# An attention kernel stores 1/std in rows turned by DVE, and each transfer of a step waits for a mark of its own

## The chip, the cores and the metric

The kernel runs on one core of a Trainium2 chip. The metric is the device time of one execution, in microseconds (us). TensorE is called PE here, VectorE DVE, ScalarE ACT, GpSimd POOL, and SyncE SP; SP only issues transfers.

## What is computed

`x` has 16 sequences of 1024 tokens with 512 features. It is layer-normed, and the result goes into two branches that are added to `x`: a state-space block in chunks of 64 tokens ("attention"), and a mixture of experts in which, for each group of 32 tokens, each expert and set takes the token with the largest logit.

```python
xn = _layernorm(x)                       # (x - mean) / sqrt(var + 1e-5)
# attention branch
proj = xn @ W_in.T                       # xp, z (512 each), B, C (256 each), dt_low (16)
dt = softplus(dt_low @ dt_W.T + dt_b)
dAcs = cumsum(dt * -exp(A_log))          # within a chunk of 64
scores = einsum(C, B) * exp(dAcs_i - dAcs_j) * causal * dt_j
y = scores @ xp + C @ state * exp(dAcs) + xp * D_param   # state carried over chunks
y = y / rms(y) * norm_w * silu(z)
attn = y @ W_out.T
# expert branch, in groups of 32 tokens
logits = xn @ Wc + bc + tie
perm = logits == max over the group      # one token for each of 32 x 4 experts and sets
inner = relu(picked @ W1 + b1)
ffn = spread(inner @ W2 + b2, perm)
out = x + attn + ffn
```

## The kernel before

Three phases run one after the other, joined at their edges: attention (to about 2300 us of the span), gather (picked tokens and W1, to about 2740 us), and scatter (W2, spreading, sum). The change touches the attention phase alone.

**Steps.** The 16384 tokens are 128 tiles of 128 tokens (index n), taken two at a time in 64 steps (s, `NST`) of 256 tokens. A loop over s from 0 to 65 is written out by hand once for each engine. It works on three steps at once: step s is projected, step s - 1 scanned, and step s - 2 gated and projected out (n0 = 2s, n1 = 2(s - 1), n2 = 2(s - 2)); the first half of an iteration treats the first tile of each, the second half the second.

**1/std.** Layer norm is folded in: the projections run on the raw `x`, turned on the host (`xT`, loaded to `xr` and split into a high and a low float32r part, `xT`, by ACT `hi_x` and DVE `lo_x`), against weights whose column means were taken away at the start (`column_means`, `centre`), and their results are multiplied by 1/std on the way out of PSUM. DVE takes the statistics of a tile (`stats`, `finish_stats`), POOL makes 1/std of them (`inv_std`, four small operations, into a column of `rs`), and ACT `normalize` writes the normed tile `xn`, which SP stores for the gather phase. The logits come out with tokens along the free axis, so they need 1/std as a row on every partition: SP stores the two columns of a step to DRAM (`store_rs`, L326, token by token), waits for that to land, and loads it back to all partitions (`load_rsb`, L331). DVE `picks` (L791) uses it at the end of the step.

**PE's order in an iteration** (`tensor_program`, L1034 on): two `project_bdt` (24 matmuls together), transposes of B, `project_x(n0)`, transposes of yz, chunk states and scores of n1 (128 and short), `project_z(n0)`, `project_out(n2)`, `sums`, `scan(n1)` (L989, recorded as 128 matmuls of 32 columns, with as many weight loads); then the same for the second tiles, with `project_c` and `project_logits`, up to `scan(n1 + 1)`. The first scan waits for DVE `mask_scores(n1)` (L736) and for ACT and POOL `spread_c`.

**The rest of the iteration.** DVE: `scale_y`, `expand_c`, `gate`, `lo_x`, statistics, `lo_yz`, `states`, `mask_scores`, `residual`, `states`, and again for the second tile, then `picks(s)`. ACT: copies of the projections, `hi_x(s + 1)`, softplus, `copy_x`, `spread_c`, `normalize`, `silu_z`, `square`. POOL: `add_skip`, `inv_std`, `spread_c`, `skip_x`, `inv_rms`, `scale_b`.

**SP's order.** SP issues every transfer of the loop, in program order, and stops at each wait. The lines (L366 to L382) give: xr(s + 2), when `lo_x(s)` is done; the store of rs(s + 1); the store of xn; the store of part 0 of step s - 2, after its residual; the load of an x tile; then the load of rsb(s + 1); the store of the other xn; the store of perm, which waits for `picks(s)`; the store of part 1; and the load of the other x tile.

Of the kernel before, what the change touches and what calls it, by code (L numbers as in the profile page):

```python
# [24 lines left out]
ALU = mybir.AluOpType  # L25
# [66 lines left out]
def attention_phase(nc, io, keep, sems):  # L92
# [49 lines left out]
    rs = sb("rs", [P, NT])  # L142
# [63 lines left out]
    rs_out = sem("rs_out")  # L206
# [48 lines left out]
    rs_cols = keep["rs"].rearrange("s i p -> s p i")  # L255
# [60 lines left out]
    def sync_program(sync, gather):  # L316
# [4 lines left out]
        def load_xr(s):  # L321
            sync.dma_start(xr_place(s), io["xT"][s]).then_inc(xr_in[s % 2], 16)

        def store_rs(s):
            sync.wait_ge(ln_pool, 4 * (2 * s + 1) + 2)
            sync.dma_start(rs_cols[s], rs[:, 2 * s:2 * s + 2], allow_slow_non_contiguous=True).then_inc(rs_out, 16)  # L326

        def load_rsb(s):
            sync.wait_ge(rs_out, 16 * (s + 1))
            wait(sync, pm, 4 * (s - 2) + 1)  # L330
            sync.dma_start(rsb[:, s % 2, :], rs_rows[s].partition_broadcast(P)).then_inc(rsb_in[s % 2], 16)  # L331

        for t in range(2):
            sync.dma_start(x[:, t, :], x_dram[t]).then_inc(x_in[t], 16)
        for n, (src, _) in enumerate(stages):
            if n == 2:
                for dst, name in consts[4:]:
                    sync.dma_start(dst[:], io[name]).then_inc(const_in, 16)
# [3 lines left out]
            if n == 2:  # L342
                load_xr(0)
                sync.dma_start(x[:, 2, :], x_dram[2]).then_inc(x_in[2], 16)
                for t in range(2):
                    store_xn(t, t)
                store_rs(0)
            if n >= 2:
                sync.wait_ge(w_lo, n - 1)
            sync.dma_start(stage_view(n), src).then_inc(w_in[n % 2], 16)  # L350
        for t in range(3, 4):
            sync.dma_start(x[:, t, :], x_dram[t]).then_inc(x_in[t], 16)

        store_xn(2, 0)
        load_rsb(0)
        sync.wait_ge(w_lo, LAST_STAGE)
        load_xr(1)

        for s in range(NST + 2):
            if s == NST:  # L360
                sync.wait_ge(lg_ps, NST)
                gather["load_w1"](sync, 0)
# [3 lines left out]
            for i in range(2):  # L366
                if i == 0 and valid(s + 2):
                    sync.wait_ge(xT_lo, s + 1)
                    load_xr(s + 2)
                if valid(s + 1):  # L370
                    (store_rs, load_rsb)[i](s + 1)
                if valid(s + 1 + i):
                    store_xn(2 * (s + 1 + i) + 1 - i, 1 - i)
                if i == 1 and valid(s):
                    sync.wait_ge(pm, 4 * s + 4)
                    sync.dma_start(perm_dram[s], permT[:, s % 2, :]).then_inc(pm_out[s % 2], 16)
                if valid(s - 2):
                    sync.wait_ge(res_cp, 2 * (s - 2) + i + 1)
                    sync.dma_start(part_dram[2 * (s - 2) + i], res[:, i, :].rearrange("p (k c) -> p k c", k=KD)).then_inc(res_out[i], 16)
                if valid(s + 2):  # L380
                    n = 2 * (s + 2) + i
                    sync.dma_start(x[:, n % (2 * STB), :], x_dram[n]).then_inc(x_in[n % (2 * STB)], 16)  # L382

    def gpsimd_program(pool, gather):
        for col, value in ((ones, 1.0), (mhalf, -0.5), (ln_eps, LN_EPS), (mean, 1.0 / D)):
            nc.gpsimd.memset(col[:], value).then_inc(zeroed, 1)
        pool.wait_ge(zeroed, 4)

        def inv_std(n, j):
# [5 lines left out]
            nc.gpsimd.tensor_tensor(rs[:, n:n + 1], ve[:, j:j + 1], mhalf[:], ALU.pow).then_inc(ln_pool, 1)  # L395
            nc.gpsimd.tensor_scalar(nm[:, j:j + 1], mv[:, j, 0:1], -1.0, 1.0, ALU.mult, ALU.mult).then_inc(ln_pool, 1)
            pool.wait_ge(ln_pool, 4 * n + 3)
            nc.gpsimd.tensor_tensor(nb[:, j:j + 1], nm[:, j:j + 1], rs[:, n:n + 1], ALU.mult).then_inc(ln_pool, 1)
# [82 lines left out]
        pool.wait_ge(zeroed, 7)  # L481
        pool.wait_ge(a_ready, 2)
        inv_std(2, 0)
        gather["negate_b1"](pool)
        for s in range(NST + 2):
# [6 lines left out]
            if valid(s + 1):  # L492
                inv_std(2 * (s + 1) + 1, 1)
# [14 lines left out]
            if valid(s + 2):  # L508
                inv_std(2 * (s + 2), 0)
# [5 lines left out]
    def scalar_program(act, gather):  # L515
        def hi_x(s):
            act.wait_ge(xr_in[s % 2], 16 * (s // 2 + 1))
# [3 lines left out]
        def normalize(n):  # L521
# [3 lines left out]
                                 scale=rs[:, n:n + 1]).then_inc(xn_ready, 1)  # L525
# [28 lines left out]
        normalize(2)  # L554

        gather["cast_ident"](act)

        def copy_bdt(n):
# [3 lines left out]
            nc.scalar.activation(raw[:, n % 4, :], proj[n % 2][:, 0:C_C], ACT.Copy, scale=rs[:, n:n + 1]).then_inc(bdt_cp, 1)  # L562
# [5 lines left out]
        def copy_x(n):  # L568
# [3 lines left out]
            for c in range(2):  # L572
                rows_ = token_rows(c)
                last = nc.scalar.activation(xs[c][n % 4][rows_, :, :], proj[0][rows_, :].rearrange("p (h d) -> p h d", h=H), ACT.Copy,  # L574
                                            scale=rs[rows_, n:n + 1])
            last.then_inc(x_cp, 1)

        def silu_z(n):
            act.wait_ge(z_ps, n + 1)
            wait(act, yz_cp, n - 3)  # L580
            nc.scalar.activation(sz[:, n % 4, :], proj[1 - n % 2][:], ACT.Silu, scale=rs[:, n:n + 1]).then_inc(z_cp, 1)
# [29 lines left out]
        for s in range(NST + 2):  # L611
# [28 lines left out]
            if valid(s + 1):  # L640
                normalize(2 * (s + 1) + 1)
# [23 lines left out]
            if valid(s - 1):  # L665
                spread_c(n1 + 1)
            if valid(s):
# [7 lines left out]
            if valid(s + 2):  # L675
                normalize(2 * (s + 2))

    def vector_program(dve):
# [26 lines left out]

        def centre(n):
# [20 lines left out]
        def mask_scores(n):  # L727

            wait(dve, zeroed, 7)
# [27 lines left out]
        def scale_y(n):  # L757
# [7 lines left out]
                                           rs[:, n:n + 1], gain, ALU.mult, ALU.mult).then_inc(yt_cp, 1)  # L765
# [47 lines left out]
        for n in range(LAST_STAGE):  # L813
# [4 lines left out]
            if n == KD // 2 - 1:  # L818
# [4 lines left out]
                stats(2)  # L823
                finish_stats(2)
        dve.wait_ge(const_in, NCONST)
        for s in range(NST + 2):
# [28 lines left out]
            if valid(s + 2):  # L855
                stats(2 * (s + 2))
# [828 lines left out]
```

## Time and profile before

| | us |
|---|---|
| median of 3 runs | 3283.34 |
| lowest and highest | 3260.25, 3297.9 |
| the profiled execution | 3270.6 |
| its span, first to last instruction | 3268.5 |
| PE busy | 2973.3 (91%) |
| DVE, ACT, POOL busy | 2319.2, 1704.2, 1363.1 |

The span is that of the profiled execution, 2.1 us shorter than its time. PE busy is not PE at its peak: matmuls overlap and their ends are modelled. "PEclk" is the share of full speed (2.4 GHz) that was granted; the lower level is half (1.2 GHz). A wait "<- issue" is idle time that nothing in the profile ends. DMA shares are busy shares of the core's 16 DMA engines.

### The profile page before, as it was taken

What the parts mean: (1) busy time and instruction counts of PE and PEld (TensorE: products, weight loads), DVE (VectorE), ACT (ScalarE), POOL (GpSimd) and SP (SyncE); (2) the same over time, 40 slices, a digit from 0 to 9 for tenths busy, and PEclk for the clock granted to TensorE, in tenths of its full rate; (3) what the DMA queues carried; (4) which work ended last, traced back from release to release, by engine and by line L of the source; (5) the groups of instructions that cost most, each with busy time, mean ns of one, the idle gap of its engine ahead of it and who ended that gap; (6) DMA issues with size and microseconds to landing.
All of it is one profiled execution on the core that took longest, in us unless ns stands there. A gap on an engine that the chain in (4) does not pass through costs nothing.

```text
span 3268.5 us, 134252 instructions
## 1 busy us (share of the span) xinstructions
PE 2973.3 (91%) x59304; PEld 2525.5 (77%) x59304; DVE 2319.2 (71%) x3557; ACT 1704.2 (52%) x3678; POOL 1363.1 (42%) x2286
## 2 busy tenths in 40 slices
PE   4999999999999999999999999999788777999999
PEld 3778877877877878878778788787566666888887
DVE  2777877777877788878768788777444445777775
ACT  2555555555555565655655565555333332555555
POOL 1555565555565565655655565555100001000000
PEclk7999999999999999999989999999899998999999
DMA  4332332222222233232322322222644444778775
GB/s 113 69 65 64 76 65 63 72 66 67 75 64 65 65 74 68 72 70 66 74 64 62 72 70 76 68 60 64 212 120 114 122 120 134 221 210 234 222 208 160
DMA packets 372388, 328.94 MB, mean 101 GB/s; under 512 B 71761, under 2 KB 293457, under 8 KB 370913
## 3 DMA queue, kind: packets, MB, share of 16 engines
q1 hardware_dynamic: 371168, 320.15, 36.9%
q8 instruction: 469, 7.68, 1.1%
q14 instruction: 111, 0.90, 0.3%
q10 hardware_dynamic: 640, 0.20, 0.0%
HBM read 206.96 MB, written 113.31 MB: 98 GB/s over the span
## 4 chain that ended last, share of the span: by engine, by line
PE 75%; DVE 12%; issue 8%; POOL 2%; DMA 2%; ACT 0%; SPq 0%; DVEq 0%; POOLq 0%; ACTq 0%
PE a_proj L878 33%; PE s_rt L1548 7%; PE a_mix L878 6%; PE a_scan L989 5%; PE g_pick_ps L1294 5%; PE s_w_ps L1518 4%; DVE scan_in L736 4%; PE s_rt L1561 4%; DVE xs L754 4%; DVE g_picked L1261 3%; PE a_scan L966 2%; PE g_acc_ps L1315 2%; PE a_scan L953 2%; PE a_mix L941 2%; PE a_misc L1007 1%
## 5 line engine op out<-in xcount | busy, mean ns | idle before, releaser
L754 DVE TENSOR_SCALAR xs<-gs,mg 64x128 f32<-64x128 f32 x960 | 529.3, 612 | 8.8
L878 PE MATMUL a_proj<-wdh,xTh 128*128 128x512 f32 x1024 | 442.5, 432 | 11.2 <-DVE wdl L687 9.1
L878 PE MATMUL a_proj<-wdl,xTh 128*128 128x512 f32 x1024 | 422.2, 412 | 4.7 <-issue 4.7
L878 PE MATMUL a_proj<-wdh,xTl 128*128 128x512 f32 x1024 | 420.1, 410 | 2.4 <-issue 2.4
L1484 ACT COPY s_res<-s_rt 128x512 f32<-128x512 f32 x512 | 263.0, 600 | 279.5 <-PE s_rt L1548 279.5
L1497 DVE TENSOR_TENSOR s_resT<-s_w_ps,s_b 128x1024 f32<-128x1024 f32 x252 | 296.7, 1220 | 141.7 <-PE s_w_ps L1518 141.7
L425 POOL TENSOR_TENSOR yv<-yt,dx 128x512 f32<-128x512 f32 x128 | 211.5, 1653 | 440.2 <-DVE yt L763 438.3
L736 DVE COPY_PREDICATED scan_in<-mask,a_scan 64x512 f32<-64x512 uint32 x512 | 378.5, 739 | 16.0
L574 ACT ACTIVATE xs<-a_proj,rs 64x512 f32<-64x512 f32 x256 | 174.8, 683 | 322.7 <-PE a_proj L878 317.1
L417 POOL TENSOR_TENSOR dx<-xs,d_row 64x512 f32<-64x512 f32 x256 | 329.1, 1286 | 15.2
L598 ACT ACTIVATE scan_in<-CT,hsel 64x128 f32<-64x128 f32 x1024 | 326.1, 388 | 4.8
L1261 DVE COPY g_picked<-g_pick_ps 128x1024 f32<-128x1024 f32 x128 | 156.7, 1224 | 225.5 <-PE g_pick_ps L1294 225.5
L989 PE MATMUL a_scan<-xs,scan_in 128*32 128x32 f32 x16384 | 195.7, 200 | 115.5 <-issue 93.5
L989 PEld LDWEIGHTS a_scan<-xs,scan_in 128*32 128x32 f32 x16384 | 170.8, 110 | 137.4 <-issue 101.9
L408 POOL TENSOR_TENSOR scan_in<-CT,hsel 64x512 f32<-64x512 f32 x256 | 269.1, 1051 | 10.2 <-issue 0.2
L1239 ACT COPY g_picked<-g_pick_ps 128x1024 f32<-128x1024 f32 x128 | 129.6, 1013 | 251.0 <-PE g_pick_ps L1294 250.4
L562 ACT ACTIVATE raw<-a_proj,rs 128x272 f32<-128x272 f32 x128 | 62.4, 488 | 378.7 <-PE a_proj L878 378.7
L1548 PE MATMUL s_rt<-s_ident,s_resT 128*128 128x128 f32 x2048 | 255.5, 278 | 0.0
L878 PEld LDWEIGHTS a_proj<-wdh,xTh 128*128 128x128 f32 x1024 | 205.0, 200 | 64.8 <-issue 15.5
L878 PEld LDWEIGHTS a_proj<-wdh,xTl 128*128 128x128 f32 x1024 | 205.0, 200 | 50.7 <-issue 3.9
L1548 PEld LDWEIGHTS s_rt<-s_ident,s_resT 128*128 128x128 f32 x2048 | 219.9, 141 | 30.6 <-issue 25.4
L878 PEld LDWEIGHTS a_proj<-wdl,xTh 128*128 128x128 f32 x1024 | 206.2, 201 | 42.4 <-issue 6.6
(134 smaller groups left out, 6953.3 us busy)
## 6 DMA issues: line engine op xcount, KB each, us to landing
x<-in_x_dram SPq DMA_DIRECT2D x128, 256.0 KB, 3.0
xn_dram<-xn SPq DMA_DIRECT2D x128, 256.0 KB, 2.3
part_dram<-res SPq DMA_DIRECT2D x128, 256.0 KB, 2.5
g_xn<-xn_dram SPq DMA_DIRECT2D x128, 256.0 KB, 3.0
s_w<-in_w_dram SPq DMA_DIRECT2D x128, 256.0 KB, 3.9
s_part<-part_dram SPq DMA_DIRECT2D x128, 256.0 KB, 3.6
out_dram<-s_out SPq DMA_DIRECT2D x128, 256.0 KB, 2.9
xr<-in_xT_dram SPq DMA_DIRECT2D x63, 512.0 KB, 4.1
```

The costliest lines, as they stand in the source:

```text
L408: nc.gpsimd.tensor_tensor(c_places(1, w), src, sel, ALU.mult).then_inc(cs_cp[1], 1)
L417: nc.gpsimd.tensor_tensor(dx[rows_, :], xs[c][n % 4][rows_, :, :].rearrange("t h d -> t (h d)"), d_row[rows_, :], ALU.mult).then_inc(dx_cp, 1)
L425: nc.gpsimd.tensor_tensor(yv[:], yt[:], dx[:], ALU.add).then_inc(yv_cp, 1)
L598: last = nc.scalar.activation(dst[:, :, j, :], CT[own, n % 4, :, 0:CH], ACT.Copy, scale=hsel4[own, j:j + 1])
L736: nc.vector.copy_predicated(dst, mask[rows_, :].unsqueeze(1).unsqueeze(1).to_broadcast([CH, 4, 2, CH]), src).then_inc(mt_cp, 1)
L754: nc.vector.tensor_scalar(dst, gs[rows_, q, :].unsqueeze(1).to_broadcast([CH, 2, 2 * HD]), scale0[rows_, q, :], scale1[rows_, q, :], ALU.m ...
L878: last = nc.tensor.matmul(out, lhs[a], rhs[c], start=(k == 0 and n == 0), stop=(k == nk - 1 and n == 2))
L989: last = nc.tensor.matmul(out, scan_in[c][:, h, i:i + 32], xs[c][n % 4][:, h, :], start=True, stop=True)
L1261: nc.vector.tensor_copy(picked_view(n, tq, 1), pick_view(1)).then_inc(pick_cp[1], 1)
L1484: nc.scalar.copy(res[:, n % 4, :, :], rt_bank[:, n % 3, :, :]).then_inc(res_cp, 1)
L1497: last = nc.vector.tensor_tensor(resT[m % 2][j][:, :, sets].rearrange("p n (q r) -> p n q r", r=4), w2_place(u)[:, :, :, j * GB:(j + 1) * ...
L1548: last = nc.tensor.transpose(rt_bank[:, n % 3, g, :], resT[m % 2][j][:, place, :], ident[:])
```

## The change

- `rs` is now a ring of four steps with 32 columns each, of which two are used (`inv(n)` names tile n's), zeroed at the start. Once a step DVE transposes it in 32x32 blocks into `rsT` (`turn_inv`, after `expand_c(n1)`), so that the 1/std of a tile lie in four rows of 32. `store_rs` sends those in two transfers of four rows of 128 bytes. It now runs in iteration s for step s, as `load_rsb` does; before both ran one iteration ahead.
- `xr` is loaded in halves: one when `project_bdt` of the first tile is done, the other when that of the second is.
- Each of SP's transfers has a wait of its own: x tile 2s + 3 after `project_x(2s)`, x tile 2s + 4 after `project_x(2s + 1)`, perm(s - 1) in the next iteration, between the halves of xr.
- `stats`, `inv_std` and `normalize` work in iteration s on tiles 2s + 2 and 2s + 3 instead of 2s + 3 and 2s + 4. The second `normalize` stands earlier in ACT's order, behind `spread_c(n1 + 1)`.
- At the start the weight stages 2 and 3 are loaded as soon as their buffers are free; the stores of xn 0 and 1 and the load of x tile 2 come behind them. Statistics of tile 2 move into the loop.

```diff
@@ attention_phase: tiles and semaphores @@
-    rs = sb("rs", [P, NT])
+    rs = sb("rs", [P, 4, 32])
+    rsT = sb("rsT", [P, 2, 32])
...
-    rs_out = sem("rs_out")
+    rs_turned = sem("rs_turned")
+    rs_out = [sem(f"rs_out{i}") for i in range(2)]
...
-    rs_cols = keep["rs"].rearrange("s i p -> s p i")
+    rs_quarters = keep["rs"].rearrange("s i (q t) -> s i q t", t=32)
...
+    def inv(n, rows_=slice(0, P)):
+        return rs[rows_, n // 2 % 4, n % 2:n % 2 + 1]
@@ sync_program @@
-        def load_xr(s):
-            sync.dma_start(xr_place(s), io["xT"][s]).then_inc(xr_in[s % 2], 16)
+        def load_xr(s, i):
+            sync.dma_start(xr_place(s)[:, 2 * i:2 * i + 2, :], io["xT"][s][:, 2 * i:2 * i + 2, :]).then_inc(xr_in[s % 2], 16)
...
         def store_rs(s):
-            sync.wait_ge(ln_pool, 4 * (2 * s + 1) + 2)
-            sync.dma_start(rs_cols[s], rs[:, 2 * s:2 * s + 2], allow_slow_non_contiguous=True).then_inc(rs_out, 16)
+            sync.wait_ge(rs_turned, s + 1)
+            for i in range(2):
+                sync.dma_start(rs_quarters[s, i], rsT[i:P:32, s % 2, :]).then_inc(rs_out[s % 2], 16)
 
         def load_rsb(s):
-            sync.wait_ge(rs_out, 16 * (s + 1))
+            sync.wait_ge(rs_out[s % 2], 32 * (s // 2 + 1))
...
         for n, (src, _) in enumerate(stages):
             if n == 2:
+                for i in range(2):
+                    load_xr(0, i)
...
-            if n == 2:
-                load_xr(0)
-                sync.dma_start(x[:, 2, :], x_dram[2]).then_inc(x_in[2], 16)
+            if n >= 2:
+                sync.wait_ge(w_lo, n - 1)
+            if n == LAST_STAGE:
                 for t in range(2):
                     store_xn(t, t)
-                store_rs(0)
-            if n >= 2:
-                sync.wait_ge(w_lo, n - 1)
+                load_x(2)
             sync.dma_start(stage_view(n), src).then_inc(w_in[n % 2], 16)
-        for t in range(3, 4):
-            sync.dma_start(x[:, t, :], x_dram[t]).then_inc(x_in[t], 16)
-
-        store_xn(2, 0)
-        load_rsb(0)
         sync.wait_ge(w_lo, LAST_STAGE)
-        load_xr(1)
+        for i in range(2):
+            load_xr(1, i)
...
-            for i in range(2):
-                if i == 0 and valid(s + 2):
-                    sync.wait_ge(xT_lo, s + 1)
-                    load_xr(s + 2)
-                if valid(s + 1):
-                    (store_rs, load_rsb)[i](s + 1)
-                if valid(s + 1 + i):
-                    store_xn(2 * (s + 1 + i) + 1 - i, 1 - i)
-                if i == 1 and valid(s):
-                    sync.wait_ge(pm, 4 * s + 4)
...
+            if valid(s + 2):
+                sync.wait_ge(bdt_ps, 2 * s + 1)
+                sync.wait_ge(xT_lo, s + 1)
+                load_xr(s + 2, 0)
+            if valid(s) and valid(s - 1):
+                store_perm(s - 1)
+            if valid(s + 2):
+                sync.wait_ge(bdt_ps, 2 * s + 2)
+                load_xr(s + 2, 1)
+            if valid(s):
+                store_rs(s)
+            if valid(s + 1):
+                sync.wait_ge(x_ps, 2 * s + 1)
+                wait(sync, res_cp, 2 * (s - 3) + 2)
+                load_x(2 * (s + 1) + 1)
+            if valid(s):
+                load_rsb(s)
+            if valid(s + 1):
+                store_xn(2 * (s + 1), 0)
+            if valid(s - 2):
+                store_part(s - 2, 0)
+            if valid(s + 2):
+                sync.wait_ge(x_ps, 2 * s + 2)
+                load_x(2 * (s + 2))
+            if valid(s + 1):
+                store_xn(2 * (s + 1) + 1, 1)
+            if valid(s - 2):
+                store_part(s - 2, 1)
@@ vector_program @@
+        def turn_inv(s):
+            dve.wait_ge(ln_pool, 4 * (2 * s + 1) + 2)
+            wait(dve, rs_out[s % 2], 32 * (s // 2))
+            nc.vector.transpose(rsT[:, s % 2, :], rs[:, s % 4, :]).then_inc(rs_turned, 1)
...
             if valid(s - 1):
                 expand_c(n1)
+            if valid(s):
+                turn_inv(s)
             if valid(s - 2):
                 gate(n2 + 1)
             if valid(s + 1):
                 lo_x(s + 1)
-                stats(2 * (s + 1) + 1)
-                finish_stats(2 * (s + 1) + 1)
+                stats(2 * (s + 1))
+                finish_stats(2 * (s + 1))
...
-            if valid(s + 2):
-                stats(2 * (s + 2))
-                finish_stats(2 * (s + 2))
+            if valid(s + 1):
+                stats(2 * (s + 1) + 1)
+                finish_stats(2 * (s + 1) + 1)
@@ scalar_program @@
             if valid(s + 1):
-                normalize(2 * (s + 1) + 1)
+                normalize(2 * (s + 1))
...
             if valid(s - 1):
                 spread_c(n1 + 1)
+            if valid(s + 1):
+                normalize(2 * (s + 1) + 1)
             if valid(s):
                 act.wait_ge(mg_ps, s + 1)
...
-            if valid(s + 2):
-                normalize(2 * (s + 2))
```

`inv_std`, `normalize`, `copy_bdt`, `copy_x`, `silu_z` and `scale_y` take `inv(n)` for `rs[:, n:n + 1]`; POOL's two `inv_std` move like the statistics; `xr_in` counts 32 a step; `zeroed` counts one more.

## Rows read from the trace of the kernel before

**Rows 1.** Waits of PE, steps 2 to 62 (118.5 to 2246 us): total us, times, longest us

```profile
PE a_scan L989 <- issue: 93.5, 76, 3.0
PE a_scan L989 <- DVE scan_in L736: 15.7, 42, 0.5
```

**Rows 2.** Busy time by windows, each one step but the first: us, busy us, PEclk, DMA

```profile
118.51:2245.86 2127.35, 1998.53 (x34900) 1692.68 (x34893) 1664.00 (x2864) 1224.08 (x2866) 1235.74 (x2131) 0.97 0.29 68
...
996.89:1033.12 36.23, 33.49 (x581) 28.26 (x573) 27.59 (x48) 20.07 (x47) 20.31 (x35) 0.95 0.28 66
1033.12:1071.06 37.94, 34.55 (x579) 28.95 (x572) 25.16 (x49) 20.02 (x47) 20.27 (x35) 0.91 0.27 63
1071.06:1103.62 32.56, 31.61 (x580) 26.92 (x572) 26.61 (x44) 20.08 (x47) 20.07 (x35) 1.00 0.33 74
...
1174.89:1207.86 32.97, 31.57 (x580) 26.92 (x572) 27.00 (x47) 20.09 (x47) 20.34 (x35) 1.00 0.33 72
...
1240.96:1273.04 32.08, 31.70 (x581) 27.13 (x573) 27.80 (x48) 20.10 (x47) 20.31 (x35) 1.00 0.30 74
```

**Rows 3.** Timeline of PE in the first scan of a step: start us, us

```profile
1011.34 1.25 PE L989 MATMUL a_scan<-xs,scan_in 128*32 128x32 f32 x123 [0.35 <-DVE scan_in L736]
1014.53 0.19 PE L989 MATMUL a_scan<-xs,scan_in 128*32 128x32 f32 x1 [1.94 <-issue]
```

**Rows 4.** Busy time by windows, at that scan and behind it

```profile
1011.30:1015.40 4.10, 1.68 (x129) 1.47 (x129) 2.64 (x6) 2.01 (x4) 2.95 (x6) 1.00 0.82 138
1015.40:1020.00 4.60, 4.60 (x16) 3.58 (x16) 2.83 (x5) 0.22 (x1) 1.97 (x3) 0.65 0.30 48
```

**Rows 5.** DMA queues of the whole run (the page): transfers, MB, share of 16 engines

```profile
q8 instruction: 469, 7.68, 1.1%
```

**Rows 6.** DMA queues, 1047.5 to 1051.5 us, the first scan of the next step

```profile
q8 instruction: 1, 0.02, 5.0%
```

**Rows 7.** DMA queues, 1021.5 to 1024.5 us, with nothing else under way

```profile
q8 instruction: 1, 0.02, 1.9%
```

**Rows 8.** DMA queues, 2213 to 2215 us, beside the stores of perm and part

```profile
q1 hardware_dynamic: 679, 0.44, 78.1%
q8 instruction: 1, 0.02, 3.0%
```

**Rows 9.** DMA queues, 1006.5 to 1010.5 us, behind a store of rs

```profile
DMA packets 1, 0.01 MB, mean 2 GB/s; under 512 B 0, under 2 KB 0, under 8 KB 0
...
q14 instruction: 1, 0.01, 4.8%
```

**Rows 10.** Timeline of SP in the step from 996.89 us

```profile
1004.65 0.38 SPq L326 DMA_DIRECT2D rs_dram<-rs  x1
1009.85 0.38 SPq L319 DMA_DIRECT2D xn_dram<-xn  x1
1012.10 0.36 SPq L379 DMA_DIRECT2D part_dram<-res  x1
...
1013.10 1.97 SPq L331 DMA_DIRECT2D rsb<-rs_dram  x1
```

**Rows 11.** Waits of SP, 118.5 to 2246 us

```profile
SPq L331 <- DMA rs_dram<-rs: 15.9, 11, 3.1
```

**Rows 12.** Timeline of SP at the start of the kernel

```profile
23.51 0.56 SPq L326 DMA_DIRECT2D rs_dram<-rs  x1
24.12 1.01 SPq L350 DMA_DIRECT2D stage<-in_w_dz_dram  x2
```

**Rows 13.** DMA data rate from 20 to 42 us in 40 slices of 0.55 us

```profile
GB/s 0 0 0 0 0 0 261 291 290 189 149 223 313 60 0 30 30 30 45 45 15 15 30 60 15 104 45 134 164 253 447 447 387 402 253 45 0 0 0 0
```

**Rows 14.** Waits of PE, whole run

```profile
PE a_scan L1021 <- DMA stage<-in_w_dz_dram: 12.0, 1, 12.0
```

**Rows 15.** Groups of DVE, 118 to 2246 us: xcount | busy us, mean ns | idle before us

```profile
L771 DVE TENSOR_TENSOR yz<-yv,sz 128x512 f32<-128x512 f32 x122 | 85.3, 699 | 144.6 <-POOL yv L425 144.6
...
L700 DVE BATCH_NORM_AGGREGATE mv<-bst 128x2 f32<-128x6 f32 x121 | 22.0, 182 | 4.2
```

More of the change, by code:

```diff
@@ L361, in sync_program @@
                 sync.wait_ge(lg_ps, NST)
+                store_perm(NST - 1)
                 gather["load_w1"](sync, 0)
@@ L384, in gpsimd_program @@
+            if valid(s - 2):
[7 more added lines that the diff above has]
+                store_part(s - 2, 1)
     def gpsimd_program(pool, gather):
-        for col, value in ((ones, 1.0), (mhalf, -0.5), (ln_eps, LN_EPS), (mean, 1.0 / D)):
+        for col, value in ((ones, 1.0), (mhalf, -0.5), (ln_eps, LN_EPS), (mean, 1.0 / D), (rs, 0.0)):
@@ L386, in gpsimd_program @@
             nc.gpsimd.memset(col[:], value).then_inc(zeroed, 1)
-        pool.wait_ge(zeroed, 4)
+        pool.wait_ge(zeroed, 5)
         def inv_std(n, j):
@@ L480, in gpsimd_program @@
         nc.gpsimd.tensor_scalar(a_row[:], a_row[:], -1.0, 1.0, ALU.mult, ALU.mult).then_inc(a_ready, 1)
-        pool.wait_ge(zeroed, 7)
+        pool.wait_ge(zeroed, 8)
         pool.wait_ge(a_ready, 2)
-        inv_std(2, 0)
         gather["negate_b1"](pool)
@@ L492, in gpsimd_program @@
             if valid(s + 1):
-                inv_std(2 * (s + 1) + 1, 1)
+                inv_std(2 * (s + 1), 0)
             if valid(s):
@@ L507, in gpsimd_program @@
                 add_skip(n1)
-            if valid(s + 2):
-                inv_std(2 * (s + 2), 0)
+            if valid(s + 1):
+                inv_std(2 * (s + 1) + 1, 1)
             if valid(s - 1):
@@ L516, in hi_x @@
         def hi_x(s):
-            act.wait_ge(xr_in[s % 2], 16 * (s // 2 + 1))
+            act.wait_ge(xr_in[s % 2], 32 * (s // 2 + 1))
             wait(act, lg_ps, s - 1)
@@ L553, in scalar_program @@
                 nc.scalar.activation(a_row[:], a_row[:], ACT.Exp).then_inc(a_ready, 1)
-        normalize(2)
         gather["cast_ident"](act)
@@ L561, in copy_bdt @@
             wait(act, st_ps, 2 * (n - 3))
-            nc.scalar.activation(raw[:, n % 4, :], proj[n % 2][:, 0:C_C], ACT.Copy, scale=rs[:, n:n + 1]).then_inc(bdt_cp, 1)
+            nc.scalar.activation(raw[:, n % 4, :], proj[n % 2][:, 0:C_C], ACT.Copy, scale=inv(n)).then_inc(bdt_cp, 1)
         def copy_bT(n):
@@ L580, in silu_z @@
             wait(act, yz_cp, n - 3)
-            nc.scalar.activation(sz[:, n % 4, :], proj[1 - n % 2][:], ACT.Silu, scale=rs[:, n:n + 1]).then_inc(z_cp, 1)
+            nc.scalar.activation(sz[:, n % 4, :], proj[1 - n % 2][:], ACT.Silu, scale=inv(n)).then_inc(z_cp, 1)
         def copy_c(s):
@@ L727, in mask_scores @@
         def mask_scores(n):
-            wait(dve, zeroed, 7)
+            wait(dve, zeroed, 8)
             dve.wait_ge(sc_ps, 4 * n + 4)
@@ L822, in vector_program @@
                 lo_x(0)
-                stats(2)
-                finish_stats(2)
         dve.wait_ge(const_in, NCONST)
@@ L1014, in column_means @@
             cols = view[0].shape[2]
-            pe.wait_ge(zeroed, 4)
+            pe.wait_ge(zeroed, 5)
             for i in range(2):
@@ L1032, in tensor_program @@
         pe.wait_ge(wdt_lo, 1)
-        pe.wait_ge(zeroed, 7)
+        pe.wait_ge(zeroed, 8)
         for s in range(NST + 2):
```

29 lines of the change are left out of this document (15 added, 14 removed).

## Prediction

> **What bounds the kernel.** The page gives TensorE (PE) 91% of the span and the chain that ended last runs through it for 75%, so I asked first where PE stands still in the attention phase. The waits of PE between the start of step 2 and that of step 63 (61 whole steps) are in [rows 1]: 93.5 us of 128.8 idle us stand ahead of `scan` (L989), in 76 pieces, and nothing that the profile shows ends them ("issue"). DVE ends only 15.7 us. Next I cut the phase into steps at each first `a_proj<-wt,xT` matmul of the PE timeline [rows 2]. The mean step is 2127.35 / 61 = 34.87 us, but those shown lie between 32.1 and 37.9. In short ones PE is busy 31.6 to 31.7 us with a granted clock of 1.00; in the two long ones shown it idles 2.7 to 3.4 us and is also busy longer, 33.5 to 34.6 us, at 0.95 or 0.91. The second part follows from the first: after a stop inside a scan [rows 3] the granted clock goes from 1.00 to a mean of 0.65, that is, it spends 3.2 of the next 4.6 us at its lower level (1.2 GHz) [rows 4]. PE had idled for 4.10 - 1.68 = 2.4 us before it fell.
>
> **Why a scan stops.** A scan is 128 matmuls with 128 weight loads in about 1.3 us, the densest stretch of PE's program. The page's queue "q8 instruction" moved 7.68 MB in 469 transfers [rows 5]: 16 KB each, and 7.68 MB over PE's 118,608 instructions is 65 bytes apiece, so q8 is, by inference, PE's program being fetched. The length of one fetch is its share of the DMA view x 16 engines x the window. At a first scan of a step: 5.0% x 16 x 4 us = 3.2 us [rows 6]. At a quiet time: 1.9% x 16 x 3 = 0.9 us [rows 7]. So the scans stop where the fetch is slow, and what slows it must be found.
>
> Traffic alone does not: with the engines 78% busy on 512-byte stores and a load at once, a fetch took 3.0% x 16 x 2 = 0.96 us [rows 8]. And a small fetch of another engine (q14, 8 KB) took 4.8% x 16 x 4 = 3.1 us with no other packet in its window [rows 9]. What those two slow ones share is the store of `rs` issued just before: 256 single words to DRAM. SP's timeline has it at 1004.65, while `rsb`, which must wait for it to land, goes out at 1013.10, right behind x [rows 10]; in 11 steps SP stands waiting for it even then, 15.9 us in all [rows 11]. So it takes 8 us or more to land, from about 8 to 16 us into a step (996.89), and the first scan starts at 14.4 us. The start of the kernel shows it best: `rs` is stored at 23.51, two 1 MB weight loads follow at 24.12 [rows 12], and from about 27 to 34 us the data rate is 0 to 60 GB/s, between 291 before and 447 after [rows 13]; PE waits 12.0 us for these loads [rows 14].
>
> The Trainium skill ("DMA: Bandwidth & Descriptors", Specifications) says that below 512 B a transfer is read, changed and written back, and (Rules for kernel authors) that a last dimension that is not contiguous costs a descriptor for each element. By its fit (a fixed 2 us and the bytes over 436 GB/s, made for another issuing path) this 1 KB store would land in 2 us; rows 10 and 11 say 8 or more, and the measurement decides. By its 512 B the new rows of 128 B are still too short.
>
> **The change, part by part.**
> *Store of rs.* 256 words become eight rows of 128 bytes in two transfers. I take this as removing the slow stretch: 32 times fewer descriptors. Were each as slow as one of the 256 (8 us / 16 per engine = 0.5 us), eight rows over a few engines would hold two each: about 1 us, and early in the step (4 us in, by `turn_inv`), ten us ahead of the first scan.
> - Stops: PE work in a clean step is 31.63 us (mean of the three short steps in rows 2). They idle 0.4 to 1.4 us; the first scan's wait for DVE stays (0.35 us, rows 3). I take 0.87 us: 32.5 us a step, clock included. 61 x (34.87 - 32.5) = -144.6 us. Seen by its causes: 93.5 us of stops, less what stays, and the excess of PE busy, 1998.5 - 61 x 31.63 = 69.1 us, which is the clock's. Bounds: at 32.1 a step -169, at 33.1 -108.
> - Start: the weight loads leave when `w_lo` allows, about 21 and 22.3 us instead of 24.12, no longer behind two stores of `xn`. At 291 GB/s 2 MB take 7.2 us, so they land near 30 instead of 40, just as the first projections end (about 29): -10 us. The load of `xr` for step 1 starts from there too, with less ahead of it; I take -2 more. Together -12; bounds -3 (only the earlier issue) and -16.
> *turn_inv.* One 32x32 transpose of 128x32 on DVE a step, not in the trace. Nearest row: the aggregate L700, 182 ns [rows 15]; the far bound is a whole `cexp`-like operation on 128x512, 0.70 us, as L771. It comes after `expand_c`, where DVE then waits 1.2 us a time for POOL's yv (L771, 144.6 us ahead of 122) [rows 15]. Its semaphores are long up (tile 2s+1's `inv_std` was half a step before). 0 us; without that cover 61 x 0.18 = 11, at most 61 x 0.70 = 43.
> *xr in halves and loads on marks.* 64 more `xr` issues and 64 more `rs` issues of 0.4 us on SP, which in rows 10 has a pause of 4.8 us ahead of xn alone. Loads now go at 1.7, 3.3, 6.3 and about 20 us of a step, all outside the scans. `load_rsb` follows a wait for the landing of rs behind the half `xr`: behind it stands only the store of xn at 13 us, and `picks` needs `rsb` at 32 us. x tiles arrive about 15 us ahead of their statistics. 0 us.
> *Stores.* `part` of the second tile no longer waits for `picks` and so leaves at the second scan, where nothing is in flight now. By rows 8 a fetch beside such a store keeps to 0.96 us. I allow 0.13 us a step: +8 us.
> *inv_std, stats, normalize.* Same count, other tiles. The second `normalize` (0.81 us on ACT in the view of tile rs) now stands ahead of the copies of mg and C; C is wanted by the logits about 4 us later. The same for POOL and DVE, whose slots stay. 0 us; with the cover gone 61 x 0.8 = 49.
> The gather and scatter phases are untouched: 0.
>
> The skill also has a rule against this change: "DMA: Bandwidth & Descriptors", Rules for kernel authors, wants small transfers joined, since under 64 KB a DMA is mostly overhead. Two more transfers a step at its fixed 2 us would be 256 us if they were waited for one by one; here they lie beside PE's work.
>
> **Sum.** -144.6 - 12 + 8 = -148.6; 3268.5 - 148.6 = 3119.9 us of span, and with the 2.1 us around it (3270.6 - 3268.5) **3122 us**. The profiled execution lies 13 us under the median of the runs, 3283.34, inside their spread.
>
> **Rivals.**
> *A. The stops go but the clock still falls.* For: nothing in a trace says what else the clock answers to. Against: rows 4 and the short steps, at 1.00 throughout. Then 69.1 us stay: 3191 us. Chance 8%.
> *B. The change does not cure the fetch,* because the slow fetches come from the stores of xn and part, which stay at 13 and 15.2 us beside the first scan. For: the stores are beside it in every first scan. Against: rows 8, 9 and 13. Then only the start is won: 3271 - 12 = 3259 us. Chance 12%.
> *C. Slower.* As B, and the store of part now does at the second scan what it does at the first. Place: scan(n1+1); price: the same 34.87 - 32.5 = 2.37 us a step, x 61 = +145 on B: 3403 us. It decides from the point at which a fetch beside a store takes over some 2 us instead of 1. Chance 5%.
> *D. The move of normalize or turn_inv reaches the path,* +43 to +49 on the forecast: 3165 to 3171 us, inside the range. Chance 5%.
>
> **Chances and range.** Forecast 70%, its own range 3090 to 3160 (bounds of the steps -169 and -108, of the start -3 and -16). With D and A I reach 3190: **3090 to 3190** holds a little over 80%. Faster by over 1% (a bound that a measurement of this kernel can still tell from no change: its runs spread 1.2%): forecast, A and D, 83%, and a part of B, which lies 0.7% under the median: 84%. Within 1%: 11%. Slower: 5%.
>
> **What the profile after would show.** Right: "PE a_scan L989 <- issue" falls from 93.5 to under 15 us; steps between 32 and 33.2 us at a clock of 0.99 or 1.00; q8 fetches in the first scan about 1 us; `rsb` follows the rs stores by under 5 us; column means (L1021) wait some 2 us instead of 12.0. Rival B would show the L989 row unchanged with fetches of 3 us; C two stops a step; A, few stops and a clock of 0.97. I would be wrong above all if rows 9 and 13 are coincidence, or if 128-byte rows are as slow as words: then the slow stretch only moves, to 4 to 12 us of the step.

## The result, and the profile after

| us | before | after |
|---|---|---|
| median of 4 runs each, on one chip | 3276.21 | 3075.21 |
| lowest and highest | 3260.25, 3297.9 | 3070.59, 3076.71 |
| span of the profiled execution | 3268.5 | 3071.6 |
| start of step 2 to start of step 63 | 2127.35 | 1946.84 |

The ratio is 0.938, 95% interval 0.932 to 0.944: faster by 6.2%. The forecast was 3122 us, its range 3090 to 3190; the kernel came out 15 us below the range. The sign and the mechanism were right, the size was 47 us short.

The waits of PE in the same 61 steps as [rows 1], from the profile after (columns: tile and line <- what ended the wait: us in total, times, longest). L1018 is now the line of `scan`.

```profile
PE a_scan L1018 <- DVE scan_in L765: 20.5, 54, 0.8
PE a_scan L1018 <- issue: 3.9, 5, 1.4
PE a_misc L1036 <- issue: 0.8, 1, 0.8
PE a_proj L907 <- issue: 0.6, 2, 0.4
```

The stops inside and ahead of the scans with no releaser have gone from 93.5 us to 3.9. What is left, some 0.38 us in 54 of 61 steps, is the first scan waiting for DVE's last mask. The phase and three steps of it, the view of [rows 2] after:

```profile
100.96:2047.80 1946.84, 1921.05 (x34897) 1640.11 (x34892) 1702.36 (x2929) 1219.37 (x2867) 1237.23 (x2136) 1.00 0.26 74
994.33:1026.77 32.44, 31.90 (x579) 27.07 (x573) 28.06 (x49) 20.08 (x47) 20.33 (x35) 1.00 0.25 73
1026.77:1058.59 31.82, 31.45 (x579) 26.88 (x573) 28.07 (x49) 19.98 (x47) 20.32 (x35) 1.00 0.25 76
1058.59:1090.40 31.81, 31.43 (x578) 26.86 (x572) 27.97 (x50) 19.99 (x47) 20.32 (x35) 1.00 0.26 74
```

The mean step is 1946.84 / 61 = 31.92 us instead of 34.87, and 43 of the 61 lie within 0.15 us of 31.8. PE idles 25.8 us instead of 128.8 in the phase, and is busy 1921.1 instead of 1998.5: of 180.5 us, 103.0 are waits and 77.5 are busy time, most of it matmuls that no longer run at the lower clock: the granted clock of the phase is 1.00. A fetch of PE's program beside the first scan and the next one, some 5 us later (the DMA view of 1042 to 1045 and of 1047 to 1050 us after, to be read as [rows 6]; 3.3% x 16 x 3 = 1.6 us and 2.0% x 16 x 3 = 1.0 us):

```profile
q8 instruction: 1, 0.02, 3.3%
...
q8 instruction: 1, 0.02, 2.0%
```

SP's timeline in one step after (994.33 on), to be held against [rows 10]:

```profile
998.76 1.02 SPq L336 DMA_DIRECT2D rs_dram<-rsT  x2
1000.63 0.33 SPq L331 DMA_DIRECT2D x<-in_x_dram  x1
1001.08 0.35 SPq L341 DMA_DIRECT2D rsb<-rs_dram  x1
1007.30 0.38 SPq L325 DMA_DIRECT2D xn_dram<-xn  x1
```

`rsb`, which waits for rs to land, follows it by 2.3 us, where it took 8.5 before. And at the start of the kernel, the waits of PE up to 101 us (compare [rows 14]):

```profile
PE a_misc L1026 <- POOL dA L486: 8.4, 2, 6.4
...
PE a_scan L1050 <- DMA stage<-in_w_dz_dram: 1.0, 1, 1.0
```

12.0 us of waiting for w_dz have become 1.0; step 2 starts at 100.96 instead of 118.51, 17.5 us earlier. What follows the start of step 63 takes 1023.8 us instead of 1022.6.

### The profile page after: what moved, and what is told of

Its sections match the earlier page's. It is cut to its first block, busy times and chain, and to the rows that moved or that the text cites. A ratio compares the mean times of both kernels' runs of the same rounds, so it can differ in the third digit from the quotient of the medians.

```text
span 3071.6 us, 134631 instructions
## 1 busy us (share of the span) xinstructions
PE 2892.8 (94%) x59304; PEld 2470.2 (80%) x59304; DVE 2356.3 (77%) x3621; ACT 1698.7 (55%) x3678; POOL 1363.6 (44%) x2287
## 4 chain that ended last, share of the span: by engine, by line
PE 79%; DVE 14%; issue 4%; POOL 1%; DMA 1%; SPq 0%; DVEq 0%; ACT 0%; ACTq 0%; POOLq 0%
PE a_proj L907 34%; PE s_rt L1577 8%; PE a_mix L907 6%; PE g_pick_ps L1323 5%; DVE scan_in L765 5%; PE a_scan L1018 5%; PE s_w_ps L1547 4%; DVE xs L783 4%; PE s_rt L1590 4%; DVE g_picked L1290 3%; PE a_scan L995 3%; PE g_acc_ps L1344 2%; PE a_scan L982 2%; PE a_mix L970 2%; PE a_misc L1036 1%
## 5 line engine op out<-in xcount | busy, mean ns | idle before, releaser
L783 DVE TENSOR_SCALAR xs<-gs,mg 64x128 f32<-64x128 f32 x960 | 564.8, 648 | 8.8
L907 PE MATMUL a_proj<-wdh,xTh 128*128 128x512 f32 x1024 | 421.7, 412 | 9.1 <-DVE wdl L710 9.1
L907 PE MATMUL a_proj<-wdh,xTl 128*128 128x512 f32 x1024 | 402.5, 393 | 0.4 <-issue 0.4
L907 PE MATMUL a_proj<-wdl,xTh 128*128 128x512 f32 x1024 | 402.6, 393 | 0.0
L907 PEld LDWEIGHTS a_proj<-wdh,xTh 128*128 128x128 f32 x1024 | 193.4, 189 | 56.4 <-issue 11.1
L907 PEld LDWEIGHTS a_proj<-wdh,xTl 128*128 128x128 f32 x1024 | 193.3, 189 | 44.2 <-issue 1.2
L907 PE MATMUL a_proj<-xTh,wth 128*128 128x256 f32 x768 | 222.2, 289 | 0.0
L907 PEld LDWEIGHTS a_proj<-wdl,xTh 128*128 128x128 f32 x1024 | 193.7, 189 | 32.4 <-issue 0.2
L907 PE MATMUL a_mix<-woh,ygh 128*128 128x512 f32 x512 | 208.9, 408 | 9.5 <-DVE ygl L804 9.5
```

What stands on the lines that cost most here:

```text
L783: nc.vector.tensor_scalar(dst, gs[rows_, q, :].unsqueeze(1).to_broadcast([CH, 2, 2 * HD]), scale0[rows_, q, :], scale1[rows_, q, :], ALU.m ...
L907: last = nc.tensor.matmul(out, lhs[a], rhs[c], start=(k == 0 and n == 0), stop=(k == nk - 1 and n == 2))
```

## Experiments

The kernel before does not take the same time on every chip: in three groups of runs it had medians of 3372, 3302 and 3299 us, while the changed kernel and its variants whose added stores did no harm lay between 3066 and 3078. Variants are therefore compared with each other, by total and by mean step (step 2 to step 63), and a ratio to before is given only with the before of its own group.

### The rows alone: r1

The kernel before with the rows and `turn_inv`, rs stored and loaded one iteration later (and a longer ring for it); SP's order, the waits, whole xr, statistics and `normalize` as before.

```diff
-            sync.dma_start(rs_cols[s], rs[:, 2 * s:2 * s + 2], allow_slow_non_contiguous=True).then_inc(rs_out, 16)
+            for i in range(2):
+                sync.dma_start(rs_quarters[s, i], rsT[i:P:32, s % 2, :]).then_inc(rs_out[s % 2], 16)
...
-                if valid(s + 1):
-                    (store_rs, load_rsb)[i](s + 1)
+                if valid(s):
+                    (store_rs, load_rsb)[i](s)
```

> The kernel before with one part of the change: 1/std goes out as eight turned rows, four tiles of SP's order as before (whole xr, x and rsb loads right behind the store of part, perm ahead of part 1); the store of rs and the load of rsb run one iteration later. Theory W (the store of single words slows every fetch of PE's program for about 8 us): the stops of the first scan go although the loads still run beside it; steps of 31.9 to 32.2 us instead of 34.9, start some 8 us shorter, span 3080 to 3100 us, ratio to before 0.94 to 0.945. Rival M (the marks, that is, loads moved away from the scans, bring it): steps stay near 34.9, ratio over 0.985.

Measured: 3088.28 us (3073.6 to 3095.5), ratio 0.915 (0.912 to 0.918). Waits of PE in its 61 steps:

```profile
PE a_scan L1002 <- DVE scan_in L747: 18.8, 49, 0.8
PE a_scan L1002 <- issue: 7.5, 7, 2.7
PE a_proj L891 <- issue: 5.2, 5, 1.6
```

The mean step is 32.07 us, and 31.94 in the changed kernel with whole xr (r8, below) on the same chip: the rows alone bring all but some 8 us of what the change brings in the steps, with SP's order as it was. The forecast of the steps held (31.9 to 32.2 us); the ratio is lower than the 0.94 expected because before took 3371.5 us on this chip. The start tells a second thing. With the rows, and no store of words among the weight loads, w_dz is waited for 3.2 us instead of 12.0, and step 2 starts at 106.5 us instead of 118.5.

### The words alone put back: r2

The changed kernel with the 256 words in place of the eight rows, at the new place, about 3.7 us into the step.

```diff
-            for i in range(2):
-                sync.dma_start(rs_quarters[s, i], rsT[i:P:32, s % 2, :]).then_inc(rs_out[s % 2], 16)
+            sync.dma_start(rs_cols[s], rs[:, s % 4, 0:2], allow_slow_non_contiguous=True).then_inc(rs_out[s % 2], 32)
```

> The changed kernel with the 256 single words back, at the new place of the store (3.7 us into a step); all marks as changed. Theory W: the slow stretch lies from about 4 to 12 us, ahead of the first scan (14.5 us), over the short matmuls of states and scores (6.6 to 7.9 us): stops there of 0.3 to 0.8 us a step, 3090 to 3130 us, rsb issued at 11 us or later instead of 6.7. Rival M: 3075 us as the changed kernel. Rival P (such a store costs the same wherever it stands): 3240 us or more.

Measured: 3231.6, 3245.3 and 3255.7 us, and 3281.4 in a fourth run (the median of the first three is used below); steps of 34.76 us. My forecast of 3090 to 3130 was wrong: I had thought that a word store over by 13 us of the step, ahead of the first scan, would do little. What came is what the rival had, 3240 us or more. PE's waits, and DVE's timeline in the step from 408.5 us:

```profile
PE a_scan L1017 <- DVE scan_in L764: 77.3, 57, 4.7
PE a_scan L1017 <- issue: 60.9, 33, 3.0
```

```profile
415.81 0.69 DVE L803 TENSOR_TENSOR ygl<-a_mix,ygh 128x512 fp32r<-128x512 f32 x1 [0.52 <-ACT ygh L631]
422.25 0.43 DVE L774 TENSOR_TENSOR gs<-a_scan,xs 64x256 f32<-64x256 f32 x1 [5.75 <-remote]
```

The words went out at 412.16 and `rsb` could leave at 422.49, over 10 us later. DVE stood for 5.75 us. The DMA view of the stretch in which it stands, 418 to 421.4, has no fetch at all, though the DMA engines are busy for only 22.9% of it; in 421.5 to 424.5 there is one of the 8 KB queue, 4.2% x 16 x 3 = 2.0 us:

```profile
q1 hardware_dynamic: 67, 0.13, 22.9%
...
q14 instruction: 1, 0.01, 4.2%
```

So fetches are not only slow, they first *start* late. This holds for all steps. In the changed kernel 32 of PE's fetches start 8 to 10 us into a step and 39 of the small ones at 9 to 11 us (counted over the steps from the records); with the words at 3.7 us not one of either starts between 7 and 11 us, and 21 and 43 start at 11 to 15. That PE's stops hang on its fetches shows best here: of its 36 stops of over 0.5 us with no releaser, 34 end 1.2 to 1.5 us behind the end of a fetch. In before the link is looser: 49 of 68 such stops have a fetch under way.

DVE's stop is something else. `gs` waits for PE's chunk scores. The last of them ended at 416.3 us, but the semaphore by which PE tells of them was raised between 418.1 and 422.2 us, and the fetch above was still under way when DVE went on at 422.25. The waits of DVE and ACT that a semaphore ended long after its matmul are marked "remote" in the view:

```profile
DVE gs L774 <- remote: 61.5, 14, 6.0
ACT BT L588 <- remote: 15.7, 10, 2.5
```

In all 14 of DVE's stops the scores had ended 7.9 us into the step and PE's semaphore came 3.4 to 6.1 us behind them. In before, where the words go out later, it is the scan's semaphore that comes late, again 14 times:

```profile
DVE yt L763 <- remote: 25.0, 14, 3.2
```

Such rows stand in the views of before and of r2, r3, r4, r9 and r11, the kernels with words next to each other, and in none of the changed kernel, r1, r5 to r8, r10 and r12. The words thus act in two ways, and r2 has both: its first scans wait 77.3 us for DVE's masks instead of some 21, which are these 14 stops, and 60.9 us with no releaser, where PE waits for its own program. Why PE's semaphores come late, no run tells.

### Words added to the kernel that does not need them: r3

The changed kernel with a needless store of 256 words a step, about 7.7 us into it, where before had its own.

```diff
+            sync.dma_start(keep["spare"].rearrange("s i p -> s p i")[s], wmat[:, 0:2], allow_slow_non_contiguous=True).then_inc(spare_out[s % 2], 16)
```

> The changed kernel with its rows, and beside them a store of 256 single words of a constant to a DRAM tensor that nobody reads, once a step at the place where the kernel before had its store (when 1/std of the next step's first tile is made, about 7.7 us into a step). It is work added, the output stays. Theory W: the stops of the first scan come back, steps of 34 to 35 us, fetches of 3 us, 3220 to 3270 us. Rival M: 3075 to 3085 us.

Measured: 3220.9 us (3217.6 to 3224.2), steps of 34.25 us.

```profile
PE a_scan L1029 <- issue: 70.7, 55, 4.3
PE a_scan L1029 <- DVE scan_in L776: 21.8, 59, 0.8
```

Its phase, in the columns of [rows 2]:

```profile
103.74:2193.24 2089.50, 1981.99 (x34898) 1681.30 (x34893) 1694.82 (x2929) 1219.19 (x2867) 1235.44 (x2135) 0.98 0.27 69
```

A store that nothing waits for in time brings back the stops of [rows 1] and 147 us (3220.9 against 3073.6 of r8, in the same group). No wait for this store carries the cost; it is what the store does to what goes on beside it.

### Whole xr: r8

```diff
-            sync.dma_start(xr_place(s)[:, 2 * i:2 * i + 2, :], io["xT"][s][:, 2 * i:2 * i + 2, :]).then_inc(xr_in[s % 2], 16)
+            if i == 1:
+                sync.dma_start(xr_place(s), io["xT"][s]).then_inc(xr_in[s % 2], 32)
```

> The changed kernel with xr loaded whole again, at the mark of its second half. Theory W: no difference, 3070 to 3080 us, ratio to before 0.935 to 0.942. Rival: the halves matter because one 512 KB load holds the queues longer than two of 256 KB; then over 15 us slower.

Measured: 3073.63 us (3070.4 to 3077.8), steps of 31.94 us: as against 3075.2 us and 31.92 of the changed kernel, which ran in another group of runs. No gain or cost of the halves shows.

### What makes the words slow: r4, r5, r6, r7, r10

Five needless stores at r3's place. r3 stores 256 words in two rows, each word 4 bytes from the next. r4 stores 128 words 4 bytes apart; r5 256 words to SBUF, two in each partition and 8 bytes apart; r6 128 pairs of words, 8 bytes apart; r7 128 rows of 32 bytes; r10 128 words 512 bytes apart.

```diff
@@ r4 @@
-spare=nc.dram_tensor("spare_dram", [NST, 2, P], F32, kind="Internal").ap()
-keep["spare"].rearrange("s i p -> s p i")[s], wmat[:, 0:2]
+spare=nc.dram_tensor("spare_dram", [NST, 1, P], F32, kind="Internal").ap()
+keep["spare"].rearrange("s i p -> s p i")[s], wmat[:, 0:1]
@@ r5 @@
+spare_sb[:, 0:4:2], wmat[:, 0:2]
@@ r6: [NST, P, 2] @@
+keep["spare"][s], wmat[:, 0:2]
@@ r7: [NST, P, 8] @@
+keep["spare"][s], ident[:, 0:8]
@@ r10: [NST, P, P] @@
+keep["spare"][s][:, 0:1], wmat[:, 0:1]
```

> The changed kernel with 128 needless single words a step stored to DRAM at the place where the run with 256 of them had them (about 7.7 us into the step, behind the load of rsb). The theory that each tiny DRAM write has its own price: half the words, half the time to land (about 4 us instead of 7.3 to 8.1), over by about 12 us into the step, before the first scan at 14.4, so that few scans stop: mean step 31.9 to 32.6 us, total 3075 to 3120 us. The rival that any such store costs a fixed time, however many words: as with 256 words, steps of 34.2 us and 3220 us.

> The changed kernel with 256 needless single words a step, issued at the same place as in the run with 256 words to DRAM, but written to SBUF. If it is the writes to DRAM that are slow, this costs nothing: land within 3 us, steps of 31.9 us, 3070 to 3085 us. If it is the number of 4-byte pieces by itself, wherever they go: steps of 34.2 us and 3220 us.

> The changed kernel with a needless store of 128 pairs of words (8 bytes each, 1 KB in all) to DRAM at the same place: half as many pieces as the run with 256 words, the same bytes. Price by the piece: as with 128 words, landing in about 4 us, steps 31.9 to 32.6 us, 3075 to 3120 us. Price by the bytes written: as with 256 words, 34.2 us a step and 3220 us.

> The changed kernel with a needless store of 128 rows of 32 bytes (4 KB in all) to DRAM at the same place. Price by the piece: as with 128 words, landing in about 4 us, 3075 to 3120 us. Price by the bytes written: four times that of 256 words, over 3300 us. If whole 32-byte rows are written without the detour that makes words slow, it lands in about 2 us and costs nothing: 3070 to 3085 us.

> The changed kernel with 128 needless single words a step to DRAM as in the earlier run with 128 words, but each word 512 bytes from the next instead of 4. If words are slow because neighbours meet in the same stretch of DRAM (each write has to wait for the one before it to be read, changed and written back), spreading them cures it: landing within about 3.5 us instead of 6.9, 3070 to 3080 us. If every write under some size is slow by itself, wherever it goes: landing in about 6.9 us and 3110 us as before.

| added store | lands after, us | 8 KB fetches 2 to 4 us behind it, us | 16 KB fetches 6 to 8 us behind it, us | mean step | total |
|---|---|---|---|---|---|
| r3: 256 words | 7.6 (to 10.9) | 2.8 | 2.7 | 34.25 | 3220.9 |
| r4: 128 words | 6.9 | 2.3 | 2.0 | 32.70 | 3110.1 |
| r6: 128 pairs | 3.6 | 2.5 | 1.3 | 31.95 | 3070.8 |
| r7: 128 rows of 32 bytes | 2.9 | 0.4 | 1.1 | 31.95 | 3071.3 |
| r5: 256 words, SBUF | 3.0 | 0.4 | 1.2 | 32.01 | 3070.5 |
| r10: 128 words, spread | 2.7 | 0.5 | 1.1 | 31.94 | 3066.2 |

(Medians over the steps of the profiled execution, worked out from its records.) The page's row of the issues for r4, and the same row for r10 (last column: median us from issue to landing):

```profile
spare_dram<-wmat SPq DMA_DIRECT2D x55, 0.5 KB, 7.0
```

```profile
spare_dram<-wmat SPq DMA_DIRECT2D x57, 0.5 KB, 2.7
```

Same count, same bytes, same source, same place in the step: only the distance in DRAM differs, and with it the whole cost. (r4 and r10 ran on different chips, but that is not it: r11, below, ran on the chip of r10, and there its 256 words next to each other took 9.8 us to land.) It is not the count of pieces (r5, r10), not their size (r10), and not DRAM as such (r7). It is words that lie next to each other in DRAM. Pairs stand between: they land in 3.6 us and still slow the small fetches for some 4 us, but no time is lost by it. Of the expectations, those of r5 and r7 were met, and r10's words landed in under 3.5 us as its first theory had it (its total is 4 us below the range). My picture of a price for each word, by which half the words would take half the time, failed: r4 takes 6.9 us to land, not 4, and its step is just over the range (32.70), though its total falls inside; r6 lands in 3.6 us but costs nothing and ends below its range. That neighbours wait for one another at one place of the memory would fit all six, but it is my guess; which part of the memory path it is, no run tells.

### The place of the words in the step: r11

```diff
-                store_spare(s + 1)
                 store_xn(2 * (s + 1), 0)
...
                 store_xn(2 * (s + 1) + 1, 1)
+                store_spare(s + 1)
```

> The changed kernel with the 256 needless words a step of the run that took 3221 us, issued at about 24 us into the step (behind the second store of xn) instead of 7.7. In the changed kernel only 10 instruction fetches of 16 KB in all steps start between 25 and 32 us of a step, and 47 start in its first us, against 32 at 8 to 10 us. If the harm is that fetches wanted by a scan are late, it shrinks when none of these is near: steps 31.9 to 32.6 us, 3075 to 3120 us. If a word store harms whatever runs beside it (a fixed 2 to 3 us a step), 3220 us again.

Measured: 3172.94 us (3165.4 to 3180.5), steps of 33.70 us. Neither number was met.

```profile
PE a_scan L1029 <- issue: 48.7, 67, 2.1
PE a_scan L1029 <- DVE scan_in L776: 23.0, 57, 1.4
PE a_proj L918 <- issue: 17.3, 18, 2.4
```

The stretch of 24 to 34 us of the step meets the second scan, which ends a step, and the projections that begin the next (L918). 43.1 us of the stops at the scan end 32 us or more into the step. I had counted only where fetches start and forgotten that starts are put off (and miscounted: 14 of them start between 25 and 32 us, not 10). At none of the three places tried did the words cost nothing, since fetches fall in nearly every part of a step; the harm went from 107 us (here, against r10) over 147 (r3) to 172 us (r2 by its median of 3245.3, both against r8) with what wants a fetch just then.

### The start alone: r9

The kernel before with the store of rs of step 0 behind the last weight stage.

```diff
-                store_rs(0)
...
+        store_rs(0)
         store_xn(2, 0)
         load_rsb(0)
```

> The kernel before with one thing moved: the store of rs of step 0 (256 words) goes out behind the last weight loads of the start instead of ahead of them. If it is the word store that slows the weight loads: w_dz's wait at column_means(2) falls from 12.0 to 2 to 5 us, step 2 starts some 8 to 10 us earlier (118.5 to about 109), and the steps stay at 34.9 us, so 8 to 10 us in all, under what the total's scatter shows. If the loads are slow by themselves (2 MB beside others): wait and start unchanged.

Measured: 3296.57 us (3286.8 to 3309.8) against 3299.33 us of before in its group, ratio 0.9994 (0.996 to 1.002). PE's waits up to 110 us, and SP's timeline:

```profile
PE a_misc L997 <- POOL dA L460: 17.3, 2, 15.2
...
PE a_scan L1021 <- DMA stage<-in_w_dz_dram: 3.6, 1, 3.6
```

```profile
50.79 0.43 SPq L326 DMA_DIRECT2D rs_dram<-rs  x1
51.26 0.80 SPq L319 DMA_DIRECT2D xn_dram<-xn  x1
61.98 0.33 SPq L331 DMA_DIRECT2D rsb<-rs_dram  x1
62.36 0.91 SPq L322 DMA_DIRECT2D xr<-in_xT_dram  x2
```

The wait for w_dz falls from 12.0 to 3.6 us, as I had read it from [rows 12 to 14]: the words did hold up the weights. But step 2 starts at 119.0, not at the 109 that I expected. The words, now at 50.79, take 11 us to land, and SP stands for them ahead of the load of xr: ACT waits 16.7 us for xr instead of 10.4, and PE waits 15.2 instead of 7.8 us for POOL's dA. Moved, the stop is paid at the next transfer in the queue. In the changed kernel xr goes out ahead of rs, and the rows land in 5 us (from the records).

### The wait that is left: r12

The first three of the twelve matmuls of `project_x(n0 + 1)` go ahead of the first scan of the changed kernel.

```diff
                 sums(s)
+                project_x(n0 + 1, range(1))
             if valid(s - 1):
                 scan(n1)
             if valid(s):
-                project_x(n0 + 1)
+                project_x(n0 + 1, range(1, KD))
```

> The changed kernel with the first 3 of the 12 matmuls of project_x(n0+1) put ahead of the first scan instead of all behind it. In the changed kernel 53 of 61 first scans wait some 0.38 us for DVE's last mask, with PE having nothing before them; 0.69 us of work put there covers it. If that wait is what is left on PE's path: steps of 31.5 us, 20.1 us less in all, 3050 to 3058 us against 3070 to 3077. If the scan's later start (0.31 us) makes DVE or the second scan late in turn: 3070 to 3080 us, with the wait showing elsewhere.

Measured: 3058.76 us (3056.9 to 3062.8), ratio 0.928 (0.923 to 0.933); r10, in the same group and otherwise the changed kernel with a store that costs nothing that shows, took 3066.2. The total is just above what I expected (3050 to 3058), and the step of 1942.57 / 61 = 31.85 us is not the 31.5 expected. PE's waits in the phase, and the phase itself:

```profile
PE a_scan L1020 <- issue: 7.0, 6, 1.8
PE a_proj L907 <- issue: 0.5, 2, 0.3
```

```profile
100.98:2043.55 1942.57, 1935.25 (x34898) 1636.93 (x34893) 1703.50 (x2929) 1218.79 (x2867) 1235.95 (x2135) 1.00 0.25 74
```

The 20 us of waiting for DVE are gone, and little took their place: PE idles 7.3 us in the phase instead of 25.6 in r10. But PE is busy 12.2 us longer than in r10 (1935.3 against 1923.0), so the phase gains 6.1 us (1942.57 against 1948.62) and not 20. Going from projection to scan and back happens once more a step; 12.2 / 61 = 0.2 us a step is what that costs, by the two sums; I did not measure it by itself. A small gain, and the fastest kernel of this study.

## Why the forecast was right in kind and short in size

- **What the stops come from: right.** The rows of [rows 9, 10, 13] were read as one cause, the word store. r1 (rows in, steps of 32.07 us), r3 (words in, 147 us lost) and r2 show it from both sides. That all of it goes by way of PE's program fetches was too narrow: PE's late semaphores, which the prediction did not have, carry a part: 56 of the 119 us that PE idles longer in r2 than in r8. In before they cost DVE 25.0 us, but PE waits for DVE's masks only 15.7 us there, so little of it can be theirs. Rival B (the stores of xn and part) and with it C fall: those stores are unchanged in place in r1.
- **The clock: right.** Rival A said 69.1 us of busy time would stay; 77.5 us went, those and 8.5 more. In r3 the busy time rose by 60 us (against r8) with 71 us of stops at the scans, in r4 by 17 (against r10) with 26. A us of such a stop thus cost another 0.6 to 0.9 us of slower matmuls behind it.
- **The clean step: the term that failed.** I took 32.5 us, that is 31.63 of work and 0.87 idle, halfway in what the three short steps of [rows 2] idled (0.4 to 1.4). It measured 31.92: 31.49 and 0.42. The 0.4 of the first scan's wait for DVE is nearly all that stays. What two of the short steps idled beyond it were stops of 0.6 and 1.0 us with no releaser, just behind the first scan, of a kind that came 9 times in the 61 steps (the row below) and not once in those after. I had left them in the floor, though they look like the cause that was to go. That is 0.45 x 61 = 27.5 us, and 8.5 us more in busy time (31.63 against 31.49, not explained further). The bound that I kept for it, 32.1, was itself too high: the shortest step before, with its mask wait and a granted clock of 1.00, should have been the centre, not the edge. Most steps now lie just under the 32 to 33.2 us that I had named as a sign of being right.

```profile
PE a_scan L953 <- issue: 4.7, 9, 1.0
```

- **Part at the second scan: +8 us, measured 0.** I had allowed for it without a row of such a stop. PE does not stop there; a fetch beside 512-byte stores takes 1.3 us on the mean, 1.8 at most, and that is soon enough.
- **The start: -12 us, measured -17.5.** The weights came as forecast (wait 12.0 to 1.0). With the rows alone (r1) step 2 starts 12.0 us earlier, and in r8, on the same chip, another 4.5: what goes beyond the forecast comes from the other parts of the change, SP's new order at the start above all, and it was not taken apart further. r9 shows one piece of it: behind the words xr came late.
- **turn_inv, halves, marks, normalize: 0 us, right.** r8 for the halves, as far as it goes; the transposes take 0.20 us in a gap of DVE's, and D's 43 to 49 us show nowhere. The tail added 1.2 us.

3119.9 - 27.5 - 8.5 - 8 - 5.5 + 1.2 = 3071.6, the span measured.

- **How the words act: half right.** I described a stretch in which a fetch is slow (3 us for 1). r2 shows that fetches wanted in it also start 3 to 4 us late, and that PE's semaphores come late. That fits words ahead of a scan being as bad as words beside it, and I would have been wrong had the change only moved them.
- **Size and number of the pieces.** The Trainium skill ("DMA: Bandwidth & Descriptors", Specifications) has a store below 512 B read, changed and written back. By it the pieces of r6, r7 and r10 and the rows of 128 bytes are all of the slow kind; none of them cost the kernel time here. Its rule to join small transfers (same page, Rules for kernel authors: under 64 KB a transfer is mostly overhead) speaks against rows in two transfers; no run here has them joined. The prediction counted the halves of xr with them, but these are of 256 KB, and the rule does not reach them. Its fixed 2 us, a fit for the other issuing path, is near what r7, r10 and the rows took (2.1 to 2.9), and far from the 7 to 11 of adjacent words. The measurement decides.

## What to carry to other kernels

Idle time that no releaser explains, in the densest part of an engine's program, is a question to ask of the queue that fetches the program: see what was issued in the 10 us before. A wait that ends as "remote" on one core is a second one: hold the end of the work against the time of its semaphore. A per-partition column stored word by word next to each other in DRAM is what to look for; turn it into rows first (0.2 us on DVE here), or keep the words apart. And when a slow cause is to be removed, the floor to forecast from is the best step seen less what the cause still does in it, not the mean of the good ones.

## What the hardware showed that I had not expected

- 128 words 4 bytes apart take 6.9 us to land and slow what runs beside them; 128 words 512 bytes apart take 2.7 us and disturb nothing.
- One such store of 1 KB or less holds back more than PE's fetches: the 8 KB fetches take 2.3 to 2.8 us instead of 0.4 (r4, r3 against r7), and PE's semaphores can reach DVE late, by up to 6.1 us in r2.
- The kernel before, with such stores, took 3299 to 3372 us on three different chips (3276 in the runs of the result), and the changed kernel and the variants that did no harm 3066 to 3075: most of the spread went with them.
